# A graph layer's segment sums: the dense part shortened from 1536 to 1152 destinations, and a sparser wait in front of the gathers

## What is computed

```python
h = relu(layernorm(x))
H = gelu(h @ W1.T + b1)                        # one row per node
W_tar = gelu(H[src] @ WA.T) @ WB.T             # 4 mixing weights per edge
agg = segment_sum(H[src][:, :, None] * W_tar[:, None, :], dst)   # 128 x 4 per node
agg = gelu(agg)
out_edge = einsum('ehm,em->eh', agg[dst], W_tar)
agg_node = segment_sum(out_edge, dst) / max(count(dst), 1)
out = x + gelu(concat(agg_node, H)) @ W2.T + b2
```

## Time and profile before

| what | value |
|---|---|
| median of 3 runs | 1236.04 us (1234.14 to 1236.05) |
| profiled execution, its own time | 1235.48 us |
| its span | 1233.7 us |
| granted TensorE clock, mean over the span | 0.896 |
| TensorE busy | 1053.0 us |
| VectorE busy | 901.9 us |
| ScalarE busy | 634.3 us |
| GpSimd busy | 851.9 us |
| moved by DMA | 205.73 MB |

### The profile page before, as it was taken

The page is one execution under the profiler, slowest core; times in us unless marked ns, Lnnn a source line. Parts: engine busy times, 40 slices in busy tenths (PEclk is TensorE's granted clock), DMA queues, the critical chain, the costliest instruction groups (busy, mean ns, idle before and its releaser), DMA issues.

```text
span 1233.7 us, 26415 instructions
## 1 busy us (share of the span) xinstructions
PE 1053.0 (85%) x7416; PEld 743.9 (60%) x7416; DVE 901.9 (73%) x2876; ACT 634.3 (51%) x1498; POOL 851.9 (69%) x910
## 2 busy tenths in 40 slices
PE   4957776658999998999799899889899989779987
PEld 3744333337778766677576676667676765446644
DVE  8648998884888687898487888668788866263275
ACT  6977766535455465676276667456566540000033
POOL 5437775555777777777777777777777777767445
PEclk9975666668999999999899999989899999889979
DMA  6335554447777755565655556555555667866632
GB/s 217 127 118 177 182 176 158 154 141 218 203 204 213 203 160 155 155 171 166 177 161 160 162 153 169 160 157 165 145 161 161 163 195 213 189 184 186 196 25 88
DMA packets 100422, 205.73 MB, mean 167 GB/s; under 512 B 29570, under 2 KB 48336, under 8 KB 99611
## 3 DMA queue, kind: packets, MB, share of 16 engines
q1 hardware_dynamic: 74804, 146.92, 40.0%
q0 software_dynamic: 25472, 57.11, 18.8%
HBM read 171.73 MB, written 32.22 MB: 165 GB/s over the span
## 4 chain that ended last, share of the span: by engine, by line
PE 42%; DVE 16%; POOL 13%; issue 12%; DMA 8%; ACT 5%; DVEq 3%; SPq 0%; ACTq 0%; POOLq 0%
PE ps L1581 20%; POOL q L780 13%; PE ps L1528 10%; PE ps L1547 7%; DMA q<-node_table,src_g 6%; DVE big L1338 3%; DVE big L1197 3%; PE ps L1531 2%; DVE q L1206 2%; DVE big L1184 2%; DVE mask L1172 2%; PE ps L1586 2%; DVEq L1154 2%; ACT big L823 1%; DMA out_dram<-q 1%
## 5 line engine op out<-in xcount | busy, mean ns | idle before, releaser
L780 POOL DMA_INDIRECT q<-node_table,src_g x796 | 780.5, 981 | 294.6 <-issue 214.4
L1581 PE MATMUL ps<-big,q 128*128 128x298 bf16 (+2 forms) x2940 | 528.9, 301 | 8.2 <-DMA q<-product_parts 7.6
L896 ACT ACTIVATE hot_b<-iota_b,q 128x128 bf16<-128x128 bf16 x848 | 270.0, 389 | 245.4 <-PE ps L1547 245.1
L1528 PE MATMUL ps<-mask,q 128*128 128x96 f32 x1592 | 275.2, 300 | 93.5 <-DVE mask L1172 90.3
L1581 PEld LDWEIGHTS ps<-big,q 128*128 128x128 bf16 x2940 | 267.9, 99 | 110.1 <-DMA q<-product_parts 7.7
L1528 PEld LDWEIGHTS ps<-mask,q 128*128 128x128 f32 x1592 | 236.3, 209 | 147.1 <-DVE mask L1172 133.4
L1206 DVE TENSOR_SCALAR q<-iota_a,q 128x294 bf16<-128x294 f16 (+2 forms) x848 | 238.1, 324 | 38.2 <-issue 22.8
L1547 PE MATMUL ps<-q,hot_b 128*128 128x294 bf16 (+2 forms) x848 | 211.2, 334 | 45.1 <-DVE big L1197 37.6
L1197 DVE TENSOR_TENSOR big<-big,ps 128x294 f32 (+2 forms) x411 | 225.9, 550 | 19.5 <-PE ps L1547 17.9
L1172 DVE TENSOR_TENSOR mask<-eq,q 128x192 f32<-128x192 bf16 x398 | 141.2, 356 | 121.6 <-DMA q<-node_table,src_g 106.0
L1184 DVE TENSOR_TENSOR big<-big,ps 128x120 f32 x398 | 110.1, 277 | 81.1 <-DVE big L1184 42.3
(11 more groups left out here) (145 smaller groups left out, 658.9 us busy)
## 6 DMA issues: line engine op xcount, KB each, us to landing
q<-product_parts SPq DMA_DIRECT2D x245, 388.0 KB
product_parts<-big SPq DMA_DIRECT2D x24, 776.0 KB, 3.5
q<-node_table,src_g POOLq DMA_INDIRECT x796
node_table<-big SPq DMA_DIRECT2D x12, 280.0 KB, 3.1
big<-node_table SPq DMA_DIRECT2D x24, 140.0 KB, 2.2
own_part<-big SPq DMA_DIRECT2D x12, 256.0 KB, 3.2
out_dram<-q SPq DMA_DIRECT2D x12, 256.0 KB, 2.0
big<-own_part SPq DMA_DIRECT2D x2, 1024.0 KB, 6.5
```

Of the source, the lines that this page charges most:

```text
L780: pool.indirect_dma_start(out=ring[:, t % R, :], out_offset=None, in_=table, in_offset=bass.IndirectOffsetOnAxis(ap=src_g[:, t:t + 1], axi ...
L896: last = nc.scalar.activation(hot_b[:, b % 2, i, :], iota_b[:, :], ACT.Abs, bias=nkey_b[:, t:t + 1])
L1528: nc.tensor.matmul(o[:, 0:MIX * W], ring[:, s + t, 0:D], mask[:, b, t, :, :], start=(t == 0), stop=(t == G - 1))
L1581: last = nc.tensor.matmul(ps[:, 3 + m, 0:n], cb[:, LEAD + P * (MIX * part + m):LEAD + P * (MIX * part + m + 1)], counts[k % 2][:, a, c0:c1 ...
```

## The change

The dense part ends at destination 1152 instead of 1536. Five chunks of at most 344 columns with the lowest take the place of six, and four product stages the place of five; `S` is 4. The gathered part begins at tile 664 instead of 768, so it has 900 tiles (450 groups), 68, 98, 98, 88 and 98 groups in stages 0 to 4. The count tiles are 98, 114, 248, 278 and 0 (738 in all), and the products 268, 270, 270 and 344 columns wide in stages 1 to 4. The halves of SBUF swap their roles, which moves buffers and a piece of clearing. The fixed slots of the last stage move (19, 23, 33, 38, 41, 29). The tail has 14 tiles instead of 13. GpSimd waits before every fourth tile instead of every second, for one group more. Core of the diff; left out are assertions, buffer addresses and the renamed halves:

```diff
--- before
+++ after
@@ -23,17 +23,17 @@
 EPS = 1e-5
 RSQRT_BITS = 0x5F3759DF
 
-EDGE = [0, 100, 400, 698, 996, 1294, 1536]
+EDGE = [0, 72, 344, 614, 884, 1152]
 K = len(EDGE) - 1
 WIDE = [EDGE[k + 1] - EDGE[k] for k in range(K)]
-FROM = [0, 190, 388, 516, 617, 705]
-TO = [204, 404, 528, 630, 717, 781]
-GSZ = [4, 2, 2, 2, 2, 1]
-CWS = [6, 6, 8, 10, 10, 6]
+FROM = [0, 160, 360, 482, 580]
+TO = [176, 374, 496, 596, 678]
+GSZ = [4, 2, 2, 2, 1]
+CWS = [6, 6, 8, 10, 6]
 CW = max(CWS)
 S = K - 1
 LOWEST = EDGE[2]
-PITCH = [max(WIDE[2::2]), LOWEST]
+PITCH = [max(LOWEST, max(EDGE[1] + w for w in WIDE[1::2])), max(WIDE[2::2])]
 SW = max(WIDE[2:])
 GROUPS = [(TO[k] - FROM[k]) // GSZ[k] for k in range(K)]
 ORDER = list(range(K - 1, -1, -1))
@@ -46,7 +46,7 @@
 
 D0 = EDGE[K]
 DT = D0 // P
-G0 = 768
+G0 = 664
 G1 = 1564
 G = 2
 W = 24
@@ -58,8 +58,9 @@
 TP = 2 * (D + MIX)
 NP = 1 + SPL * MIX
 SLOT = PL * W
-KEYED = {K - 1: 1, K - 2: 1, K - 3: 2, 0: 3, K - 4: 4, K - 5: 5}
-KEY_AT = {(1, 2): K - 3, (1, 18): 0, (2, 18): K - 4, (3, 18): K - 5}
+KEYED = {K - 1: 1, K - 2: 1, K - 3: 2, 0: 3, K - 4: 4}
+KEY_AT = {(1, 2): K - 3, (1, 18): 0, (2, 18): K - 4}
+KEY_SETS = max(KEYED.values())
 KEY_LAG = 8
 AHEAD = 2
 EV = MIX + 2
@@ -77,8 +78,8 @@
 WROWS = MIX * SPL
 
 PRE = 2 * HALVES
-GATHERS = [50, 52, 76, 78, 78, 64]
-LOW_GROUPS = [0, 0, 24, 22, 5, 0]
+GATHERS = [68, 98, 98, 88, 98]
+LOW_GROUPS = [0, 0, 28, 16, 0]
 assert sum(GATHERS) == NG and len(GATHERS) == S + 1 and DT * P == D0
 assert sum(LOW_GROUPS) == GROUPS[0] and len(LOW_GROUPS) == S + 1
 
@@ -157,7 +158,7 @@
 
 
 def half(k):
-    return k % 2 if k else 1
+    return (k + 1) % 2 if k else 0
 
 
 def first_column(k):
...
@@ -499,9 +503,10 @@
         def x_part(c):
             return next(i for i in range(XP) if 4 * c < XQ[i + 1])
 
-        ETILES = [(a, a + 4) for a in (12, 16, 20, 24, 28, 32, 36, 4, 8)] + [(40, 44), (44, 48), (0, 4), (48, NT)]
+        ETILES = [(a, a + 4) for a in (12, 16, 20, 24, 28, 32, 36, 4)] + [(DT, 12), (8, DT)]
+        FIRST_LATE = len(ETILES)
+        ETILES += [(40, 44), (44, 48), (0, 4), (48, NT)]
         NE = len(ETILES)
-        FIRST_LATE = 9
         GELU = [c for c in range(NE) if ETILES[c][0] >= DT]
         NGELU = len([c for c in GELU if c < FIRST_LATE])
         assert sorted(a for c in range(FIRST_LATE) for a in range(*ETILES[c])) == list(range(SPLIT // P, CUT // P))
...
@@ -625,17 +630,18 @@
                 if s == S and a == 9:
                     sp.wait_ge(dense_stored, 32 * (S - 1))
                     sp.dma_start(w2a_sb, w2t[:, 0, :]).then_inc(ld_w2a, 16)
+                if s == S and a == 19:
                     sp.wait_ge(added, CUT_GROUP)
                     sp.dma_start(sums_d[:, D0:CUT], acc[0:NP, MIX, 0:CUT - D0]).then_inc(early_sums_stored, 16)
-                if s == S and a == 13:
+                if s == S and a == 23:
                     sp.wait_ge(early_sums_stored, 16)
                     sp.dma_start(sums_e, sums_d[:, SPLIT:CUT].rearrange("r (p a) -> p r a", a=NE_))\
                         .then_inc(early_sums_loaded, 16)
-                if s == S and a == 23:
+                if s == S and a == 33:
                     sp.wait_ge(early_weights_ready, 1)
                     sp.dma_start(weights_d[:, SPLIT:CUT].rearrange("r (p a) -> p r a", a=NE_),
                                  parts_e.rearrange("p m s a -> p (m s) a")).then_inc(early_weights_stored, 16)
-                if s == S and a == 28:
+                if s == S and a == 38:
                     sp.wait_ge(early_weights_stored, 16)
                     sp.dma_start(weights_e, weights_d[:, SPLIT:CUT]).then_inc(early_weights_loaded, 16)
                 if s == S and a == 18:
@@ -775,8 +781,8 @@
             for t in range(TG):
                 if t == 2:
                     pool.memset(c3[:, :, :, 0:LEAD], 0.0).then_inc(lead_zeroed, 1)
-                if t >= R and t % G == 0:
-                    pool.wait_ge(group_summed, (t - R) // G + 1)
+                if t >= R and t % (2 * G) == 0:
+                    pool.wait_ge(group_summed, min((t - R) // G + 2, NG))
                 pool.indirect_dma_start(
                     out=ring[:, t % R, :], out_offset=None, in_=table,
                     in_offset=bass.IndirectOffsetOnAxis(ap=src_g[:, t:t + 1], axis=0),
...
@@ -945,6 +951,7 @@
                     act.wait_ge(row_stored[1], 16 * (NCH // 2))
                     act.wait_ge(t_split, NCH)
                     wipe(t0[0], TAIL[0] + TAIL[1])
+                    wipe(WORK1, WORK_WORDS)
                 if s == 0 and slot.at == 0:
                     high_parts(0)
                 if s == 0 and slot.at % 2 == 0 and slot.at // 2 + 1 < HALVES:
@@ -955,8 +962,8 @@
                     nc.scalar.activation(c3[:, h % PBUFS, 0:pair_size(h), LEAD + MIX * D:LEAD + 2 * MIX * D],
                                          cf[:, h % FBUFS, 0:pair_size(h), :, :].rearrange("p a m d -> p a (m d)"),
                                          ACT.Copy).then_inc(part_mid, 1)
-                if s == S and slot.at >= 12 and slot.at % 3 == 0 and (slot.at - 12) // 3 < NGELU:
-                    c = GELU[(slot.at - 12) // 3]
+                if s == S and slot.at >= 19 and (slot.at - 19) % 3 == 0 and (slot.at - 19) // 3 < NGELU:
+                    c = GELU[(slot.at - 19) // 3]
                     act.wait_ge(added, CUT_GROUP)
                     nc.scalar.activation(agg(c, 0, MIX), agg(c, 0, MIX), ACT.Gelu).then_inc(ga_ready, 1)
                 if s == 1 and slot.at == 0:
...
@@ -1347,7 +1354,7 @@
                                             cf[:, h % FBUFS, 0:pair_size(h), :, :].rearrange("p a m d -> p a (m d)"),
                                             c3[:, h % PBUFS, 0:pair_size(h), LEAD + MIX * D:LEAD + 2 * MIX * D],
                                             ALU.subtract).then_inc(part_lo, 1)
-                if s == S and slot.at == 20:
+                if s == S and slot.at == 29:
                     v.wait_ge(early_sums_loaded, 16)
                     make_weights(sums_e, parts_e, early_weights_ready, link, chained)
                 if s == S and slot.at == 24:
...
```

More of the change, by code:

```diff
@@ L216, in gnn_kernel @@
         acc = at(ACC0, PL * NA).rearrange("p (m n) -> p m n", m=PL)
-        dn = at(0, MIX * D0).rearrange("p (m n) -> p m n", m=MIX)
-        assert MIX * D0 <= HALF and NT * D <= ACC0 - HALF
-        QW = CB * CROW // 2 + R * ROW + CTT + -(-CTT // 2) + HA * NT * CW // 2 + MIX * SW
+        dn = at(HALF, MIX * D0).rearrange("p (m n) -> p m n", m=MIX)
+        assert MIX * D0 <= ACC0 - HALF and NT * D <= HALF
+        STAGE_WORDS = max(MIX * SW, max(5 * (TO[k] - FROM[k]) + GROUPS[k] for k in range(K)),
+                          3 * max(TO[k] - FROM[k] for k in range(K)) + NG)
+        QW = CB * CROW // 2 + R * ROW + CTT + -(-CTT // 2) + HA * NT * CW // 2 + STAGE_WORDS
         q = sb("q", [P, QW])
@@ L271, in gnn_kernel @@
         newton = work[:, 11, 6 * NT:7 * NT]
-        WORK1 = HALF + 12 * 512
+        assert HALF + 12 * 512 <= ACC0
+        TAIL = [2 * 4 * ROW, 32, GC * P]
+        TAIL0 = ACC0 + PL * NA - sum(TAIL)
+        WORK_WORDS = 5 * P + 3 * NT
+        WORK1 = TAIL0 - 2 * GC - WORK_WORDS
         ident = pro(WORK1, P)
@@ L330, in gnn_kernel @@
         most_r = q[0:1, KEY0 + 2 * ET:KEY0 + 2 * ET + P]
-        assert KEY0 + 2 * ET + P <= STAGE0 + MIX * SW
+        assert KEY0 + 2 * ET + P <= STAGE0 + STAGE_WORDS
         FR = max(CGG, NG)
-        frow = [big[0:1, MIX * D0 + FR * i:MIX * D0 + FR * (i + 1)] for i in range(2)]
-        assert MIX * D0 + 2 * FR <= HALF
+        frow = [big[0:1, HALF + MIX * D0 + FR * i:HALF + MIX * D0 + FR * (i + 1)] for i in range(2)]
+        assert MIX * D0 + 2 * FR <= ACC0 - HALF
         acc_g = at(0, PL * NACC).rearrange("p (m n) -> p m n", m=PL)
@@ L536, in count_wait @@
             if k == 0:
-                return 2
+                return NAB
             r = (K - 1 - k) // 2
@@ L935, in _ @@
                         act.wait_ge(sums_checked, s - 2)
-                    act.wait_ge(keys_ready, min(s + 1, 5))
+                    act.wait_ge(keys_ready, min(s + 1, KEY_SETS))
                     evacuate(b, stage)
                     if b >= 3:
-                        clear(b % 2, NT - AB, NT, first_column(b))
+                        clear(half(b), NT - AB, NT, first_column(b))
                 while made < batches and first_slot[made] <= i + 2:
@@ L970, in _ @@
                     act.wait_ge(unit_done, NT * (s - 1) + a1)
-                    clear(k % 2, a1 - AB, a1, first_column(k))
+                    clear(half(k), a1 - AB, a1, first_column(k))
             act.wait_ge(unit_done, NT * S)
@@ L1313, in _ @@
                     v.wait_ge(counts_added, CGG)
-                    nc.vector.tensor_reduce(most_p[:, b:b + 1], counts[1][:, AB * b:AB * b + AB, :], axis=AX.XY,
+                    nc.vector.tensor_reduce(most_p[:, b:b + 1], counts[0][:, AB * b:AB * b + AB, :], axis=AX.XY,
```

(4 more changed lines are left out.)

21 lines of the change are left out of this document (9 added, 12 removed).

## The result

The changed kernel takes 1362.53 us, the median of 4 runs (1360.43 to 1365.27), against 1235.29 us for the kernel before in the same job. The ratio is 1.1027, with a 95% interval of 1.1008 to 1.1046: slower by a tenth, 5.5 us above the forecast and inside its range. The profiled execution took 1365.27 us, the longest of the four, with a span of 1363.5 us, 129.8 us more than before; by the medians the difference is 127.2 us.

The account below looks back on a forecast made before the run. GpSimd, issuing a gather every 1.262 us, was taken as the bound behind stage 0, VectorE's loop with a low-clocked TensorE in it. 85.8 + 32 + 5 - 2.2 + 1 = 121.6; with 1235.5, 1357 us; range 1335 to 1384.

Parts of the forecast that it names:

- R3: Rival: TensorE's products set the stages, so fewer products give 83 us less, 1153 us; chance 0.02.
- R4: Rival: new tile ranges miss a destination and the general path runs, over 3200 us; chance 0.01.
- Later gathers: Behind stage 0: 68 more gathers left to issue at GpSimd's 1.262 us each, on the path throughout, +85.8 us.
- The wait: GpSimd's wait on every fourth tile: removed waits return nothing, the earlier demand costs 2.5 us at two hiccups, +5 us.
- R2: Rival: the new wait idles GpSimd at every fourth tile, +30 to +55 us instead of +5, 1382 to 1407; chance 0.09.
- Stage 0: First stage: 18 more groups and 22 more count tiles, +32 us, between estimates of 26.2 and 40 us.
- the lower of the two sums: Stage 0 estimate from lengths of slot pairs: 18 groups at 0.70 and 22 counts at 0.62 us, 26.2 us.
- R1: Rival: stage 0 absorbs its 32 us in VectorE's gaps and a faster TensorE clock, 1340 or 1325 us; chance 0.10.
- The last units: Six product units after the last gather, on the path, shrink by 344/400: -2.2 us.
- Removed products: One product stage of 49 units, 384 of 1536 columns, lies beside gathers and so gives 0.
- the moved steps: Steps moved to other slots of the last stage, on SP, ScalarE and VectorE, cost 0.
- the tail: End of the kernel, 58.0 us: a fourteenth tile with the same columns in all, +1 us (0 to 3).

Follow-up runs that it names:

- a_skip2: The changed kernel with 796 instead of 900 indirect DMAs, all work of the other engines kept: 1268.03 us, ratio 1.0235 to the kernel before.
- a_wait2: The changed kernel with the old wait, before every second gather: 1354.36 us, ratio 1.0934 to the kernel before.
- b_s0_68_2: The kernel before with 18 gather groups moved from stages 1 to 4 into stage 0: 1210.94 us, ratio 0.9768 to the kernel before.

## Why the prediction was right

**The bound** was named rightly. A gather interval of 1.26 to 1.28 us holds in the middle stages of every undisturbed kernel but `a_skip2`, a third of the products makes no difference, and 104 gathers less give 98 us back. R3 is out by that, and R4 by the time itself, which is far from 3200 us. The rule of the Trainium skill that spoke for R3 ("DMA: Bandwidth & Descriptors", Anatomy of one DMA: descriptor generation small and variable) does not hold for these gathers: each keeps GpSimd busy for 0.94 us, and 104 fewer gave 98 us back.

**Later gathers, +85.8 us.** `a_wait2` has this term without the new wait: from the end of stage 0 to the last gather 951.0 us against 874.0, +77.0. It had 66 more gathers left where I had 68 (152 were out at 318.8 us), 83 us; and its real stalls were 9.6 us against 18 before.

```profile
322.61 0.94 POOL L786 DMA_INDIRECT q<-node_table,src_g  x1 [5.24 <-PE ps L1538]
...
1138.33 0.94 POOL L786 DMA_INDIRECT q<-node_table,src_g  x1 [1.77 <-PE ps L1538]
...
1186.19 0.94 POOL L786 DMA_INDIRECT q<-node_table,src_g  x1 [2.53 <-PE ps L1538]
...
1192.22 0.94 POOL L786 DMA_INDIRECT q<-node_table,src_g  x1 [1.21 <-PE ps L1538]
```

That is all of them behind stage 0. That a wider slot leaves more room at each hiccup, which I had left out, is how I read it; no run shows it by itself.

**The wait, +5 us,** was 11 us, of which about 2 lie in stage 0. The two errors (8.8 too much, 6 too little) nearly cancelled, so the 86.7 us of the table agree with 90.8 better than the terms do: that agreement is luck, and in part the whole sum's is too, since the 4 us too much here stand against 7.7 too little in stage 0 and 4.5 in the last units. R2, its price of 30 us and more, did not come.

**Stage 0, +32 us,** was 39.7 us (37.5 in `a_wait2`). In size that is the end that I kept as the upper bound, 40 us by TensorE's busy time at its low clock, and busy TensorE grew by 45 us there. But TensorE was busy for 177 of the 238 us and VectorE for 193, and no run shows which of them set the pace. The groups of the changed kernel's stage 0, answering to the earlier trace rows:

```profile
L786 POOL DMA_INDIRECT q<-node_table,src_g x152 | 164.7, 1083 | 75.3 <-issue 41.6 <-PE ps L1538 30.7 <-DMA own_part<-big 3.0
L1543 PE MATMUL ps<-zero 128*128 128x512 bf16 x147 | 79.0, 604 | 0.0
L1535 PE MATMUL ps<-mask,q 128*128 128x96 f32 x280 | 77.6, 430 | 35.2 <-DVE mask L1179 34.4
...
L1554 PE MATMUL ps<-q,hot_b 128*128 128x294 bf16 x98 | 41.1, 419 | 20.6 <-DVE big L1204 14.3 <-ACT hot_b L905 5.5
```

GpSimd still waits 30.7 us there, so it was not the bound, as forecast. The mean duration of a gather fell from 1121 to 1083 ns: 152 x 1083 - 114 x 1121 = 36.9 us for 38 gathers, 0.97 us each, nearly the 0.94 of the earlier trace rows. This agrees with the rule of the Trainium skill ("GPSIMD Engine Reference", Specifications) by which the long ones belong to the two-input instructions of line 1338, whose number did not change. By `b_s0_68_2` the 18 groups are 15.9 us (0.70 us each was assumed), which leaves 37.5 - 15.9 = 21.6 us for 22 count tiles, 0.98 against the 0.62 that I took from a single pair. That pair, 262.50 to 270.86 us in the earlier trace rows, I had misread: VectorE adds three counts in it, as in most others, and not four.

```profile
265.33 0.45 DVE L1197 TENSOR_TENSOR big<-big,ps 128x294 f32 x1
...
269.46 0.46 DVE L1197 TENSOR_TENSOR big<-big,ps 128x294 f32 x1
...
270.49 0.46 DVE L1197 TENSOR_TENSOR big<-big,ps 128x294 f32 x1
```

What it has more is the mask and the sum of a third group, so its 0.62 us price no count. The 0.70 us of a group is only part of its cost too: the pair from 175.44 us has its add, while its mask and its sum stand in the pair before, 166.87 to 175.44 us, which has a fourth count as well and lasted 8.57 us. So the lower of the two sums of the prediction had no ground in its pairs. How the 38 us divide stays open, since the disturbed runs divide them otherwise. R1 is out.

**The last units** were the one term with the wrong sign, +2.3 instead of -2.2 us. Two things made it. TensorE had waited before the last sums and then ran at its low clock; the timeline of TensorE:

```profile
1286.29 1.14 PE L1535 MATMUL ps<-mask,q 128*128 128x96 f32 x4 [3.88 <-DVE big L1191]
...
1287.49 1.17 PE L1535 MATMUL ps<-mask,q 128*128 128x96 f32 x4
...
1289.07 1.07 PE L1588 MATMUL ps<-big,q 128*128 128x344 bf16 x3
...
1292.40 0.60 PE L1588 MATMUL ps<-big,q 128*128 128x344 bf16 x3
```

Three products take 1.07 us until about 1292 and 0.60 behind it (granted clock 0.85 for the stretch, against 1.00 in the earlier trace rows). And two groups were left to be summed when the last gather landed, where the kernel before had one: from the end of its issue to the first product 7.1 us passed, against 4.8. The products themselves then took 15.6 us, as long as the wider ones before, instead of the 13.4 that I took. The chain that ended last also runs through a product load, which the kernel before did not wait for:

```profile
1298.13 4.16 DMA q<-product_parts
```

But TensorE worked beside it, and stood for no more than 0.31 us:

```profile
1302.33 0.32 PE L1588 MATMUL ps<-big,q 128*128 128x344 bf16 x1 [0.31 <-DMA q<-product_parts]
```

`a_wait2` has all this too (1269.8 to 1294.3, 24.5 us, clock 0.86, and a product load of 5.62 us on its chain, for which TensorE stood 1.89 us), so it is no accident of one run. Why the load comes late was not tried. **Removed products** were worth nothing else, and the moved steps and the tail (+1.1) came as forecast.

## What to carry to other kernels

A busy share hides the gaps that belong to an engine: divide a stretch by the number of its instructions and see whether the interval ever varies. One that hardly does belongs to the likely bound, whatever TensorE's share says, and a run with fewer of them tests it. When work is divided between two methods, price the marginal unit of each at the engine that bounds the stage where it lands: here a third of all products was free to keep and a gather cost about 1.26 us, except in the one stage where its engine had slack, and moving 18 groups there won 2.3%. A coarser wait saved nothing here, as the met waits had cost nothing, and it took slots from the ring at every hiccup: 11 us.

## What the hardware showed unexpectedly

Behind stage 0, GpSimd's pace for 128-row gathers did not depend on the load: in the median 0.94 us and a gap of 0.30 us with the DMA engines at a share of 0.52 as at 0.74, and with or without a met wait in front. In two jobs waits passed about 1 us late every 6 us or so, which made each kernel that also ran undisturbed, the one before included, 15 to 17% longer; TensorE's products went on during some of the delays. Nothing in the kernels differed, and the cause is not known.
